# A fused decoder layer on one core: where the attention scores of the next unit stand in TensorE's queue

## The reference

```python
q = _layernorm(x)                                   # 4 x 1024 x 256, 16 heads of 16
energy = jnp.einsum('nqhd,nkhd->nhqk', q, k)        # k = v = ctx, 64 keys
attn = jax.nn.softmax(energy / jnp.sqrt(jnp.float32(D)), axis=-1)
out = jnp.einsum('nhqk,nkhd->nqhd', attn, v).reshape(n, -1, E)
x = x + (out @ W_out.T + b_out)
...
h = jax.nn.silu(_tlin(z, w1_w, w1_s)) * _tlin(z, w2_w, w2_s)     # z = _layernorm(x)
h = jax.nn.gelu(_tlin(h, h1_w, h1_s), approximate=False)         # 1024 -> 1024
h = jax.nn.gelu(_tlin(h, h2_w, h2_s), approximate=False)         # 1024 -> 1024
x = x + _tlin(h, w3_w, w3_s)
```

## Time and profile before

| | |
|---|---|
| time, median of 3 runs | 1079.14 us (1078.26 to 1080.61) |
| the profiled execution: its own time | 1080.7 us |
| its span on the core | 1079.0 us |
| PE busy | 958.8 us (89%) |
| PE weight loads busy | 758.9 us (70%) |
| DVE busy | 583.0 us (54%) |
| ACT busy | 555.1 us (51%) |
| POOL busy | 211.0 us (20%) |
| granted TensorE clock, mean | 0.976 |

### The profile page before, as it was taken

One profiled execution on the slowest core, in us unless ns is written; L12 is line 12 of the kernel. 1 busy time (PEld: TensorE's weight loads), 2 busy tenths in 40 slices (PEclk: granted clock), 3 DMA queues, 4 the chain that ended last, 5 costly groups with the idle time before them and its releaser, 6 DMA issues.

```text
span 1079.0 us, 15934 instructions
## 1 busy us (share of the span) xinstructions
PE 958.8 (89%) x5251; PEld 758.9 (70%) x5251; DVE 583.0 (54%) x957; ACT 555.1 (51%) x809; POOL 211.0 (20%) x239
## 2 busy tenths in 40 slices
PE   4523999867799999999999999999999999999994
PEld 2313888755677777777777777777777777777883
DVE  5698774554465455545555546465455555553231
ACT  2444776434466357536654763566366536644431
POOL 2553224720310040004002200300040013002000
PEclk9999999958899999999999999999999999999997
DMA  9540342332200210021012002100210120011010
GB/s 273 147 132 11 116 118 74 113 122 96 81 20 1 78 58 0 20 77 39 0 34 83 19 0 61 56 19 10 68 58 0 34 82 20 0 53 39 20 35 21
DMA packets 47280, 61.78 MB, mean 57 GB/s; under 512 B 9139, under 2 KB 40630, under 8 KB 47190
## 3 DMA queue, kind: packets, MB, share of 16 engines
q1 hardware_dynamic: 47158, 61.38, 18.7%
q10 hardware_dynamic: 64, 0.07, 0.0%
q0 software_dynamic: 32, 0.00, 0.0%
HBM read 46.09 MB, written 12.71 MB: 55 GB/s over the span
## 4 chain that ended last, share of the span: by engine, by line
PE 63%; DVE 8%; ACT 4%; issue 3%; DMA 1%; DVEq 0%; POOL 0%; ACTq 0%; POOLq 0%
PE pair L1141 42%; PE pair L1130 9%; PE pair L1102 3%; PE pair L1118 3%; PE pair L1091 2%; PE pair L1068 1%; PE pair L1111 1%; DVE prob L954 1%; DVE prob L962 1%; DVE red L958 1%; DVE vbuf L998 1%; DVE red L947 1%; DVE st L922 1%; ACT L818 1%; DMA flag_column<-most 1%
## 5 line engine op out<-in xcount | busy, mean ns | idle before, releaser
L863 ACT ACTIVATE vbuf<-pair,scl 128x512 f32<-128x512 f32 x128 | 87.6, 685 | 243.8 <-PE pair L1141 243.8
L1141 PE MATMUL pair<-h2hi,h2T 128*128 128x512 f32 x512 | 205.8, 402 | 0.0
L1141 PE MATMUL pair<-h1hi,h1T 128*128 128x512 f32 x512 | 204.0, 399 | 1.6 <-DVE h1lo L977 1.6
L1141 PE MATMUL pair<-h2lo,h2T 128*128 128x512 f32 x512 | 202.1, 395 | 0.0
L1141 PE MATMUL pair<-h1lo,h1T 128*128 128x512 f32 x512 | 199.9, 390 | 0.0
L1141 PEld LDWEIGHTS pair<-h1hi,h1T 128*128 128x128 f32 x512 | 96.1, 188 | 34.4 <-issue 10.5
L1141 PEld LDWEIGHTS pair<-h2hi,h2T 128*128 128x128 f32 x512 | 96.1, 188 | 28.3 <-issue 5.9
L977 DVE TENSOR_TENSOR h2lo<-vbuf,h2hi 128x512 fp32r<-128x512 f32 x64 | 44.2, 690 | 128.8 <-ACT h2hi L864 128.8
L1141 PEld LDWEIGHTS pair<-h2lo,h2T 128*128 128x128 f32 x512 | 96.1, 188 | 22.3
L1141 PEld LDWEIGHTS pair<-h1lo,h1T 128*128 128x128 f32 x512 | 96.2, 188 | 19.0
L977 DVE TENSOR_TENSOR h1lo<-vbuf,h1hi 128x512 fp32r<-128x512 f32 x80 | 57.6, 720 | 84.6 <-ACT h1hi L864 83.8
(11 more groups left out here) (137 smaller groups left out, 1750.2 us busy)
## 6 DMA issues: line engine op xcount, KB each, us to landing
sg<-in_h SPq DMA_DIRECT2D x20, 512.0 KB, 3.3
xres<-in_x SPq DMA_DIRECT2D x8, 512.0 KB, 8.8
stage<-in_h SPq DMA_DIRECT2D x8, 512.0 KB, 3.4
ring<-alpha_rows SPq DMA_DIRECT2D x16, 256.0 KB, 3.8
ring<-kernel_rows SPq DMA_DIRECT2D x16, 256.0 KB, 3.6
x_rows<-xres SPq DMA_DIRECT2D x8, 512.0 KB, 2.9
x_rows<-x1t SPq DMA_DIRECT2D x8, 512.0 KB, 2.9
xr<-x_rows SPq DMA_DIRECT2D x8, 512.0 KB, 3.8
```

Source lines behind the costliest of these rows:

```text
L863: e.activation(vb[:, s % 2, :], h_ps[s % 4], ACT.Gelu, scale=sc)
L1141: ins = e.matmul(bank, w[:, k, m * P:(m + 1) * P], src[part][:, k, :], start=(k == 0 and part == 0), stop=(k == HC - 1 and part == 1))
```

## The change

Two lists of pieces move, and nothing is added or removed. On TensorE `scores` of units 1 to 3 stand behind `turn_p` of units 0 to 2, at stages 2, 5 and 8. On VectorE `maxima` of units 1 to 3 stand behind `low` of the same stages, directly ahead of `shifted`. ScalarE, GpSimd, SyncE and the part ahead of the loop keep their order.

```diff
     TURN = [2, 5, 8, 11]
-    SCORES_AT = [1, 3, 6]
     VALUES_AT = [6, 12]
...
                 low(i, HC + s, h2 if s < HC else h1)
                 if attn and s in TURN and s != TURN[3]:
+                    maxima(j, TURN.index(s) + 1)
                     shifted(j, TURN.index(s) + 1)
-                if attn and s + 1 in TURN and s + 1 != TURN[3]:
-                    maxima(j, TURN.index(s + 1) + 1)
...
                     turn_p(j, TURN.index(s))
-                if attn and s in SCORES_AT:
-                    scores(j, SCORES_AT.index(s) + 1)
+                if attn and s in TURN and s != TURN[3]:
+                    scores(j, TURN.index(s) + 1)
                 if attn and s in VALUES_AT:
                     values(j, VALUES_AT.index(s))
```

## The result

The kernel after takes **1090.82 us** (median of four runs, 1089.38 to 1092.64), the kernel before 1078.86 us beside it (1078.26 to 1080.61). The ratio is 1.0099, with a 95% interval of 1.0084 to 1.0115: slower by 9 to 12 us. The prediction was 1087.8 us, with a range of 1084.2 to 1090.6 around it on a median of 1079.14. Against the median of before in the comparison the forecast of +8.7 us met +12.0 us, and by the ratio 0.0099 x 1078.9 = +10.7 us. The median of 1090.82 lies 0.2 us above the stated range. On the 1079.14 that the range was built on, the ratio gives 1089.8 us, inside it.

What follows compares the result with a forecast made beforehand. TensorE was taken to bound the loop except in the 12.9 us window before turn_p(0). Per turn 3.57 - 2.33 = +1.24 us, seven turns +8.7 us on 1079.14, gave 1087.8 us, range 1084.2 to 1090.6.

Steps and rivals of the forecast that it cites:

- The bound and the fixed window: From the gated step's Silu to turn_p(0): VectorE and ScalarE bound these 12.9 us, which stay; elsewhere TensorE bounds the turn.
- Scores(1) gains nothing where it stood: Stage 1: removing scores(1) gains nothing; the standstill ahead of turn_p(0) grows from 0.38 to 1.65 us.
- Units 2 and 3 nearly cancel: Scores(2) and scores(3) leaving stages 3 and 6 gain 2.33 us together, nearly cancelled by two added behind transposes.
- The cost of a scores behind transposes: Stages 2, 5 and 8: each costs 1.27 - 0.08 = 1.19 us, the restart paid once; 3.57 us a turn.
- second rival: Beside the transposes: each moved scores costs its full 1.27 us, shape change paid on both sides; +10.4 us, 1089.5 us, chance 0.09.
- The later softmax: Maxima directly ahead of shifted on VectorE: normalised(1) ends some 1.1 us later, 1.2 us left before turn_p(1); costs nothing.
- The clock: At the 1.65 us standstill: clock stays at 1.00; a rival had it fall, +6.2 us, 1094 us or more, chance 0.02.

Runs made afterwards that it cites:

- E3: The kernel after, with maxima(0) moved ahead of the last gated product on VectorE: 1082.6 us against 1080.44 of before, ratio 1.0018.
- E1: The kernel after, with scores and maxima of unit 1 put back to stage 1: 1081.76 against 1080.44 us of before, ratio 1.0014.
- e2: The kernel before, with only scores(1) moved behind turn_p(0) and maxima(1) directly ahead of shifted(1): 1087.65 against 1080.44 us, ratio 1.0068.
- e8: The kernel after, with scores over all 128 rows of contraction instead of 64 (doesn't compute the layer): 1106.66 us, one run.
- e9: The kernel before, with only maxima(1) to maxima(3) moved on VectorE to directly ahead of shifted: 1082.11 us against 1081.13, ratio 1.0008.
- e7: The kernel before, with scores over all 128 rows of contraction instead of 64 (doesn't compute the layer): 1094.05 us, one run.

## Why the prediction was right, and which term was off

**The bound and the fixed window: right.** The stretch from the Silu to `turn_p(0)` is 12.92 us before and after. E3 shows that it is the chain's length and not TensorE's work that sets it: 1.26 us out of the chain gave 1.24 us a turn. One premise was put too narrowly: `maxima(1)` is not the only reader of `scores(1)`, `shifted(1)` reads them too. It also stands behind the product in VectorE's queue, so nothing hangs on it.

**Scores(1) gains nothing where it stood: right.** The standstill grew from 0.38 to 1.71 us, 1.65 forecast, so the scores took 1.33 us where they stood and not 1.27. That doesn't enter the sum, which is counted from the start of `turn_p(0)`. E1 and e2 measure the move by itself at 1.25 and 1.28 us a turn (101.82 - 100.57, and 101.65 - 100.37).

**Units 2 and 3 nearly cancel: right.** E1 has just these two, and costs 0.20 us a turn. By the prediction's own numbers it would have been 2 x 1.19 - 2.33 = 0.05, by the measured cost beside the transposes 0.19.

**The cost of a scores behind transposes: the mis-sized term.** I took 1.27 - 0.08 = 1.19 us, on the ground that a restart is paid once when two pieces stand together, and it measured 1.26. The 0.07 us three times a turn, seven turns, are 1.5 us: +8.7 should have been +10.2, and the forecast of the time is low by that. That is nearly the second rival's figure, 1.27 and +10.4 us, by which the time would have been 1089.5. The chance of 0.09 for it was too low. The restart was read from what one kind of neighbour does, and carried to another that pays for it in another place. The second rival's reason was only half right too: the change of shape costs 0.09 us on the way in whichever neighbour it has, but e8 shows that it isn't why the pair saves nothing.

**What is left.** From 10.2 us by the turns to 10.7 by the ratio, or 12.0 by the medians, no cause is shown. The interval of 9.1 to 12.4 us holds all three. The 12.0 leans on a low median of before, 1078.86 us of four runs; beside the experiments the same kernel had 1080.44 (25 runs), 1080.98 (17) and 1081.13 (19).

**The later softmax: right for this kernel.** `normalised(1)` was put 1.1 us later and with 1.2 us left. After, its product starts at 523.98 and is 1.23 long, so it ends at 525.21, 24.77 us behind the Silu, where it was 23.63 before: 1.14 later, and 1.26 us ahead of `turn_p(1)` at 526.47:

```profile
523.98 1.23 DVE L961 TENSOR_TENSOR prob<-prob,red 128x1024 f32<-128x1024 f32 x1
```

What I missed is that the next `scores` also waits for `shifted`, which the late maxima make late. In the change it doesn't matter. In e9, at `scores(3)`, it costs 0.10 us a turn.

**The clock:** it reads 1.00 in each column group of the loop from 380 to 980 us in the kernel after; a standstill of 1.71 us leaves it at the upper level.

## What to carry to other kernels

A piece of work has two prices: what it costs where it stands, and what it costs where it goes. Before moving one on the bounding engine, look for the stretches in which that engine waits, count from the release of the wait, and treat what lies ahead of it as free. Moving a piece out of such a stretch and onto the bound costs its whole length, and moving one in gains at most the size of the standstill. To find a gain, shorten the chain that ends in the wait, by steps whose inputs are long there, or give the engine other work ahead of it, and stop at the size of the standstill, read by starts.

## What the runs showed of the hardware that I had not expected

Eight transposes start their successor 0.79 us behind their own start when it is a 512-column matmul and 0.87 when it is a 256-column one of the same shape in rows, 0.96 when that has 64 rows. A matmul behind a piece of small matmuls pays for the restart on one side or the other, so that pieces put together cost what they cost apart (2.14 against 0.88 + 1.27, and 2.60 against 0.88 + 1.73). The exception is a 64-row `scores` ahead of a `values`, 2.26 against 1.27 + 1.20, where both have a shape of their own. With full-row scores in e7 the exception is gone, 2.92 against 1.73 + 1.20. Why TensorE saves it between these two shapes no run shows.
